# A graph layer over 100,000 rows on one core: VectorE's output rows and leaky quarters interleaved with the row statistics, and the lookup's mask made by a ScalarE sign function

## The reference

```python
deg = max(segment_sum(1, dst), 1);  norm = deg ** -0.5
h = relu(layernorm(x))                               # no learned scale or shift
h_src, h_dst = h[src], h[dst]
msg = (h_src @ W1 + (h_src * h_dst) @ W2) * (norm[src] * norm[dst])   # called with deg**-0.5 as norm
h_N = segment_sum(msg, dst) + h @ W1
y = where(h_N >= 0, h_N, 0.2 * h_N)                  # leaky relu
out = x + y / max(sqrt(sum(y * y, axis=1)), 1e-12)
```

## Time and profile before

| | |
|---|---|
| runs of the kernel before | 1301.07 us median (1281.04 to 1303.91) |
| the profiled execution | 1289.29 us |
| its span, first to last instruction | 1287.6 us |
| busy: PE / PE weight load / DVE / ACT / POOL | 64% / 60% / 68% / 55% / 57% |
| mean granted TensorE clock | 0.815 of full speed |
| mean DMA traffic | 134 GB/s |

### The profile page before, as it was taken

How to read it: one execution, slowest core, us unless ns; L and a number is a source line. 1 busy time by engine, 2 the same in 40 slices (tenths; PEclk the granted TensorE clock), 3 DMA queues, 4 the chain that set the end, 5 groups by cost and what they waited for, 6 DMA issues and landing times.

```text
span 1287.6 us, 21312 instructions
## 1 busy us (share of the span) xinstructions
PE 828.3 (64%) x6102; PEld 775.7 (60%) x6102; DVE 875.9 (68%) x2731; ACT 708.0 (55%) x2944; POOL 731.8 (57%) x694
## 2 busy tenths in 40 slices
PE   0331485777678766857767767786786775788730
PEld 0320474767667666856667666775686665688730
DVE  3510386777668778776678776885886774899670
ACT  0000384755655756666567465664665754777750
POOL 0577207556666667576666756686477675423171
PEclk9965697888779788877898788887887886898865
DMA  0611023444443535445354363453443642535230
GB/s 23 237 51 51 17 87 120 138 164 132 146 155 125 187 129 176 148 139 185 117 158 167 121 205 118 135 191 124 149 171 122 200 158 88 186 115 169 113 123 31
DMA packets 68798, 172.89 MB, mean 134 GB/s; under 512 B 14378, under 2 KB 34509, under 8 KB 62429
## 3 DMA queue, kind: packets, MB, share of 16 engines
q1 hardware_dynamic: 49862, 135.41, 30.9%
q0 software_dynamic: 18816, 36.08, 8.8%
HBM read 96.89 MB, written 77.04 MB: 135 GB/s over the span
## 4 chain that ended last, share of the span: by engine, by line
PE 33%; ACT 28%; another core or an unknown queue 19%; issue 11%; DVE 4%; DMA 3%; SPq 0%; POOL 0%; ACTq 0%; DVEq 0%; POOLq 0%
ACT junk L927 14%; PE pu L1056 14%; PE pt L1046 6%; PE pt L1043 3%; ACT ct L911 3%; ACT ybuf L915 3%; PE pe_x L1024 2%; ACT hd L919 2%; PE pe_m L1081 2%; PE pe_m L1079 2%; PE pe_m L1080 2%; ACT msg L979 1%; DMA xin<-in_x 1%; ACT hs L919 1%
## 5 line engine op out<-in xcount | busy, mean ns | idle before, releaser
L1056 PE MATMUL pu<-w,ct 128*128 128x128 f32 x1568 | 263.0, 318 | 265.8 <-ACT ct L911 190.1
L1056 PEld LDWEIGHTS pu<-w,ct 128*128 128x128 f32 x1568 | 229.5, 224 | 287.2 <-ACT ct L911 202.3
L1046 PE MATMUL pt<-nident,bst 128*128 128x128 f32 x1568 | 323.4, 305 | 26.4 <-issue 25.3
L915 ACT COPY ybuf<-pu 128x512 f32<-128x512 f32 x196 | 114.3, 583 | 367.1 <-remote 193.8
L1046 PEld LDWEIGHTS pt<-nident,bst 128*128 128x128 f32 x1568 | 279.6, 220 | 33.6 <-issue 33.1
L463 POOL DMA_INDIRECT out<-oe,sstage x196 | 234.0, 1194 | 82.3 <-issue 82.3
L458 POOL DMA_INDIRECT xs<-in_x,stage x196 | 241.4, 1232 | 53.2 <-issue 53.2
L458 POOL DMA_INDIRECT xd<-in_x,stage x196 | 225.0, 1148 | 59.7 <-issue 59.7
L1043 PE MATMUL pt<-ident,xin 128*128 128x128 f32 x784 | 238.8, 305 | 26.6 <-issue 21.2
L927 ACT ACTIVATE junk<-ybuf 128x128 bf16<-128x128 f32 x784 | 230.7, 302 | 0.0
L815 DVE SCALAR_TENSOR_TENSOR xo<-ybuf,rd,xin 128x128 f32<-128x128 f32 x784 | 210.2, 344 | 0.0
(11 more groups left out here) (134 smaller groups left out, 1200.9 us busy)
## 6 DMA issues: line engine op xcount, KB each, us to landing
xin<-in_x SPq DMA_DIRECT2D x96, 512.0 KB
out<-xo SPq DMA_DIRECT2D x48, 1024.0 KB, 8.7
srow<-src_rows SPq DMA_DIRECT2D x49, 256.0 KB
edge_rows<-oe SPq DMA_DIRECT2D x49, 256.0 KB, 9.1
same<-same_segment SPq DMA_DIRECT2D x49, 128.0 KB
xs<-in_x,stage POOLq DMA_INDIRECT x196
xd<-in_x,stage POOLq DMA_INDIRECT x196
out<-oe,sstage POOLq DMA_INDIRECT x196
```

Source lines behind the costliest of these rows:

```text
L915: act.copy(ybuf[:, s.buf(), q * 512:(q + 1) * 512], pu[:, q % 2, :]).then_inc(u_evac, 1)
L1046: last = pe.matmul(pt[:, q % 2, f], mean[:, s.buf(0, 2), col:col + 1].to_broadcast([P, D]), nident[:], start=False, stop=True)
L1056: last = pe.matmul(pu[:, q % 2, f], ct[:, q % 2, f], w1[:], start=True, stop=True)
```

## The change

VectorE's work is put in another order and cut finer; one of the two masks goes to ScalarE.

- The leaky relu of a step becomes four instructions of 128 x 512, and between them stand the four edge pairs of the row statistics. `y_done` is raised at the fourth.
- The 8 pairs of row statistics of `xin` stand between the 20 output rows (after every second or third row). `bn_done` is raised at the last of them, next to `f_done`.
- The is_equal mask moves ahead of `rd`, under a semaphore of its own (`eq_done`); the guard value goes behind the counting.
- The other mask is `Sign(srow + 0.5 - first)` on ScalarE, after the relu of quarter 1 and ahead of the first copy. It is +1 or -1 instead of 1 or 0, so the tables are halved (16.0 and 0.125 for 32.0 and 0.25), the lists are shifted by one partition (run length 197 instead of 196, one more small load) and the compared value `s4` gets an offset of 1.

```diff
-            for a, at in ((0, 0), (1, 1)):
-                for lo, hi in ((0, 112), (112, P - 1)):
+            for a, at in ((0, 1), (1, 2)):
+                for lo, hi in ((0, 112), (112, P - 2)):
...
                 if has(i, 3):
                     if has(i, -1):
                         sp.wait_ge(ge_done, s())
+                        sp.wait_ge(eq_done, s())
                     load_srow(s, 3)
...
-                dve.tensor_scalar(ge[:, h, 0, :], srow[:, s.buf(d), :], first[:, 0:1], None, ALU.is_ge)
                 dve.tensor_scalar(ge[:, h, 1, :], srow[:, s.buf(d), :], first[:, 0:1], None, ALU.is_equal
-                                  ).then_inc(ge_done, 1)
+                                  ).then_inc(eq_done, 1)
...
                 if has(i, -1):
-
-                    yb = ybuf[:, s.buf(-1), :]
                     dve.wait_ge(u_evac, s() * NQ)
-                    dve.scalar_tensor_tensor(yb, yb, SLOPE, yb, ALU.mult, ALU.max).then_inc(y_done, 1)
+                for q in range(NQ):
+                    if has(i, -1):
+
+                        yb = ybuf[:, s.buf(-1), q * 512:(q + 1) * 512]
+                        last = dve.scalar_tensor_tensor(yb, yb, SLOPE, yb, ALU.mult, ALU.max)
+                        if q == NQ - 1:
+                            last.then_inc(y_done, 1)
+                    if has(i, 1):
+                        edge_pair(s, 1, q)
...
-                    out_edges(s, 0, TE)
                     if has(i, -4):
                         dve.wait_ge(out_stored[s.buf(-4)], s.dma(-4))
-                    out_dense(s).then_inc(f_done, 1)
+                for k in range(TD // 2):
+                    if has(i, -2):
+                        for t in range(k * 5 // 2, (k + 1) * 5 // 2):
+                            out_row(s, t)
+                    if has(i, 1):
+                        dense_pair(s, 1, 2 * k)
...
+            def row_signs(s, d, i=None):
+
+                act.wait_ge(srow_loaded[s.buf(d)], s.dma(d))
+                if i is None or i + d >= 2:
+                    act.wait_ge(lk_done, s(d - 1) * 2)
+                act.activation(ge[:, s.buf(d, 2), 0, :], srow[:, s.buf(d), :], ACT.Sign, bias=above[:, 0:1]
+                               ).then_inc(ge_done, 1)
...
                     relu_quarter(0)
                     relu_quarter(1)
+                if has(i, 3):
+                    row_signs(s, 3)
+                if has(i, 0):
                     if has(i, -4):
                         act.wait_ge(f_done, s(-3))
                     copy_quarter(0)
```

More of the change, by code:

```diff
@@ L116, in gnn_preln_kernel @@
         first = sb("first", [P, 1])
+        above = sb("above", [P, 1])
         ftab = sb("ftab", [P, 2, RW], F16)
@@ L248, in gnn_preln_kernel @@
         ge_done = sem("ge_done")
+        eq_done = sem("eq_done")
         lk_done = sem("lk_done")
@@ L775, in row_pair, with dense_pair, edge_pair @@
                 return dve.bn_stats(bst[:, s.buf(d, 2), at * 3:(at + 2) * 3], rows)
-            def stats_dense(s, d):
+            def dense_pair(s, d, t):
                 b = s.buf(d)
[L780 to L795, removed]
+                if t == 0:
+                    dve.wait_ge(x_loaded[b], s.dma(d))
+                if t == TD // 2:
+                    dve.wait_ge(x_loaded2[b], s.dma(d))
+                last = row_pair(s, d, t, xin[:, b, t * D:(t + 2) * D].rearrange("p (r f) -> p f r", r=2))
+                if t == TD - 2:
+                    last.then_inc(bn_done, 1)
+            def edge_pair(s, d, k):
+                e, t = s.buf(d, XBUFS), k % 2 * 2
+                if k == 0:
+                    dve.wait_ge(xs_got[e], s.dma(d, TE, XBUFS))
+                if k == 2:
+                    dve.wait_ge(xd_got[e], s.dma(d, TE, XBUFS))
+                rows = xs if k < 2 else xd
+                row_pair(s, d, TD + k * 2, rows[:, e, t:t + 2, :].rearrange("p r f -> p f r"))
             def stats_guard(s, d):
@@ L801, in stats_guard, with out_row @@
                                   EPS * NORM_MIN * NORM_MIN, ALU.mult, ALU.add)
-            def out_edges(s, first, last):
+            def out_row(s, t):
                 b, e = s.buf(-2), s.buf(-2, XBUFS)
[L806 to L813, removed]
-                    f = slice(t * D, (t + 1) * D)
-                    last = dve.scalar_tensor_tensor(xo[:, s.buf(-2, 2), f], ybuf[:, b, f], rd[:, t:t + 1],
-                                                    xin[:, b, f], ALU.mult, ALU.add)
-                return last
-            for piece in (stats_dense, stats_edges, stats_guard):
-                piece(Step(0, 0), 0)
+                if t < TE:
+                    f = slice(t * D, (t + 1) * D)
+                    dve.scalar_tensor_tensor(oe[:, b, t, :], ye[:, b, f], rd[:, TD + t:TD + t + 1], xd[:, e, t, :],
+                                             ALU.mult, ALU.add)
+                else:
+                    f = slice((t - TE) * D, (t - TE + 1) * D)
+                    last = dve.scalar_tensor_tensor(xo[:, s.buf(-2, 2), f], ybuf[:, b, f], rd[:, t - TE:t - TE + 1],
+                                                    xin[:, b, f], ALU.mult, ALU.add)
+                    if t == TD + TE - 1:
+                        last.then_inc(f_done, 1)
+            for k in range(4):
+                edge_pair(Step(0, 0), 0, k)
+            for t in range(0, TD, 2):
+                dense_pair(Step(0, 0), 0, t)
+            stats_guard(Step(0, 0), 0)
             def do(s, i):
@@ L902, in _ @@
         def _(act):
+            def row_signs(s, d, i=None):
[4 more added lines that the diff above has]
+                               ).then_inc(ge_done, 1)
+            act.wait_ge(s_ftab, 1)
+            for d in range(3):
+                row_signs(Step(0, 0), d, 0)
             act.wait_ge(dg_done, 1)
@@ L1026, in lookup @@
                 if half:
+                    pe.wait_ge(eq_done, s(d + 1))
                     for k in range(TE):
```

44 lines of the change are left out of this document (23 added, 21 removed).

## The result

The changed kernel takes 1359.71 us in the median of four runs (1357.51 to 1376.42), the kernel before 1294.67 us (1281.04 to 1303.91, four runs with one more beside the changed kernel). The ratio is 1.061, 95% interval 1.046 to 1.077: slower by some 65 us. The profiled execution took 1360.96 us, 71.7 us more than the 1289.29 us of the one before.

What follows compares the result with a forecast made beforehand. It took ScalarE's waits for a TensorE slowed by POOL's indirect DMAs to bound the kernel. The profiled 1289.3 us plus 37 (relief lost) plus 7 (steps without POOL) gave 1333 us, range 1250 to 1390.

Steps and rivals of the forecast that it cites:

- POOL without holds: POOL's indirect DMAs, no longer held by long VectorE runs: at most 1.8 us each, sum near 600 in place of 700.4.
- What the holds were worth: Steps 4 to 43: TensorE loses the pauses in which POOL was held; 40% of 92 us, +37 us.
- The block behind `dd`: VectorE waits for `dd`, then needs 8.2 us; `bn_done` 5.9 us later but covered in common steps, `f_done` hardly moves.
- +7 us in the steps without POOL: Some 8 steps where POOL rests: VectorE's own loop takes 17.5 us against 16.6, +0.9 us each.
- The sign at 0: ScalarE's mask ahead of the first copy hides in its wait for TensorE: 0 us; uncovered +29 us.
- What would show it: Signs in the profile after: ScalarE's wait ahead of copies over 367 us, third copy waiting 8 us or more in most steps.
- Nothing is lost: Rival in the loop: POOL's holds gave TensorE no relief, so only 7 us are added: 1296 us, chance 0.28.
- faster: Rival: unheld POOL ends sooner each step and frees TensorE sooner for the next transposes: 1240 us, chance 0.22.
- New waits alone: Rival: later `dd` and `bn_done` bind in all steps (44 us), sign uncovered (29 us): up to 1362 us, chance 0.08.
- the main term of the sum: TensorE, slow while POOL issues gathers, loses the relief of POOL's holds in the loop: +37 us.

Runs made afterwards that it cites:

- The kernel that keeps the order and cuts the rows: Kernel before, with leaky relu cut into quarters and output rows into groups of three by nine small extra row statistics: 1391.28 us, ratio 1.090.
- the kernel with whole rows: Changed kernel, but its 20 output rows stand in one run with the 8 row-statistics pairs behind them: 1280.45 us, ratio 0.995 to the kernel before.
- the kernel that has the order alone: Changed kernel's VectorE order, with both masks made by VectorE and the sign and its tables undone: 1366.36 us, ratio 1.063 to the kernel before.
- POOL's gathers moved aside: Changed kernel, with POOL's gathers waiting until TensorE has finished the running step's third product: 1229.64 us, ratio 0.958 to the kernel before.
- the pause: Kernel before, POOL's gathers waiting for the running step's third product: 1167.00 us, ratio 0.907; with rows and leaky relu also cut, on a faster chip, 1.012.

## Why the prediction was right, and where it was off

The forecast was slower, 1333 us in 1250 to 1390; measured were 1359.71. The direction and the mechanism were right. The size was not: against the profiled execution before I summed 37 + 7 us, and measured were 71.7.

- **POOL without holds.** Foretold: no instruction over 1.8 us and a sum near 600. Measured 633.7 us and two longer ones, both in the last steps.
- **What the holds were worth.** This is the term that I mis-sized. The full loss was 20 x (25.7 - 21.1) = 92 us, and I took 40% of it, 37, since short holds would keep part of the relief. The steps went to a mean of 25.17 us, 72 us for the 40 steps or 78% of the full loss. The bound was right and the discount wrong: of what is left of the holds, 633.7 - 588 = 46 us, 6 are in the two long instructions and the rest is in bits of at most 0.7 us, and none of the third copies waited for 2 us or more begins during one of over 1.7 us in all. The kernel that keeps the order and cuts the rows lost 2.1 us a step, 86 of the 92, its extra work included.
- **The block behind `dd`.** 8.2 us foretold, the last of it measured 8.5 us behind `dd`, and VectorE's wait ahead of `rd` 1.3 us a step. `f_done` moved by 0.2 us. That the later `bn_done` is covered in common steps is right only in the sum: in the kernel with whole rows TensorE waits 91.5 us for it and ScalarE's relus wait 84 us more, yet the whole is no slower. What covers it, TensorE's slowness or the earlier `f_done`, isn't told apart.
- **+7 us in the steps without POOL.** Not there: steps 1 and 2 (POOL is done with its burst at the start) take 17.0 and 16.6 us as before, and steps 44 to 47 together 1.5 us more. VectorE's sum of 17.5 us a step was too high, or part of it lies beside the wait.
- **The sign at 0.** Right, by the kernel that has the order alone. Its record is 723 ns and not 588.
- **What would show it.** ScalarE's wait ahead of the copies was to rise over 367 us; it fell to 356.8, and the wait for the third copy was 8 us or more in 14 steps of 40 (9 before), not in most. The loss shows in the sum with the relus, which rose from 465.5 to 502.5 us. The sign took 0.8 us a step out of that wait, which I had counted elsewhere without drawing the conclusion for this row.
- **The rivals.** "Nothing is lost" and "faster" fall with the cut rows, and the latter's argument (less POOL time frees TensorE) with them: POOL's sum fell by 67 us and TensorE was waited for longer. "New waits alone" falls with the whole rows, as far as the earlier `f_done` there lets one say. With POOL's gathers moved aside it may come back, in another kernel.

What I could not know from one trace is that the mechanism is one of the chip. That the changed kernel, too, was timed on a chip of the slow kind was luck: on the other kind the main term of the sum has nothing to stand on. The Trainium skill ("SBUF — State Buffer", Who interferes with whom) says that TensorE never waits on anyone. On two of the chips here the trace agrees, 525 and 523 matmuls beside POOL's gathers. On the others, with 66 to 73 in the same stretch, TensorE does stand while POOL issues; whether for a port of SBUF, of which that section speaks, no run tells.

## What to carry to other kernels

A stall of one engine can be what lets another one run: before a hold is cut away, look which engine advances during it. Where TensorE is waited for and its records don't show why, lay POOL's indirect DMAs beside the wait, look whether the wait ends with the last of them, and put the burst behind the work that sets the step (one semaphore wait, 9% on one kind of chip here and nothing on the other). And since the same cuts cost 9% on one chip and 1% on another (there with the pause), compare kernels on more than one.

## What the runs showed of the hardware

Of five groups of runs three came from chips on which TensorE all but stands while POOL issues gathers, and two from chips on which it doesn't; the same kernel before takes 1291 to 1301 us on the former and 1024 to 1034 on the latter. At the start of the kernel before, where hardly anything else runs, TensorE's pace beside the gathers can be read off, first its weight loads, then its matmuls and then POOL:

```profile
95.07 0.10 PEld L1028 LDWEIGHTS pe_x<-fcar,ge 128*128 128x128 f16 x1 [2.70 <-issue]
97.87 0.10 PEld L1028 LDWEIGHTS pe_x<-fcar,ge 128*128 128x128 f16 x1 [2.70 <-issue]
100.67 0.10 PEld L1028 LDWEIGHTS pe_x<-fcar,ge 128*128 128x128 f16 x1 [2.70 <-issue]
```

```profile
96.47 0.16 PE L1028 MATMUL pe_x<-fcar,ge 128*128 128x1 f16 x1 [2.48 <-issue]
99.27 0.16 PE L1028 MATMUL pe_x<-fcar,ge 128*128 128x1 f16 x1 [2.64 <-issue]
```

```profile
97.72 1.00 POOL L458 DMA_INDIRECT xs<-in_x,stage  x1 [0.31 <-issue]
99.02 0.99 POOL L458 DMA_INDIRECT xs<-in_x,stage  x1 [0.30 <-issue]
100.32 1.00 POOL L458 DMA_INDIRECT xs<-in_x,stage  x1 [0.31 <-issue]
```

A weight load every 2.80 us with one matmul between, so one instruction of TensorE in 1.40 us, its idle time marked "issue", beside a gather every 1.30 us. The profile shows nothing that it waits for. By what way POOL's issuing reaches TensorE's sequencer, and what differs between the chips, no run here tells.
